# Striking the eight largest scores of a vector with one mask over all vectors, and taking the next tile's maxima one turn earlier

## The reference, cut to what matters

```python
sim = jnp.einsum('pbnhd,hkpd->pbnhk', q, keys)      # 2 x 8 heads x 32 keys for each token
sx, ix = jax.lax.top_k(sim[0], 16)
sy, iy = jax.lax.top_k(sim[1], 16)
all_scores = (sx[..., :, None] + sy[..., None, :]).reshape(b, n, 8, 16 * 16)
scores, pk_indices = jax.lax.top_k(all_scores, 16)
```

## Time and profile before

| | |
|---|---|
| median of 3 runs | 288.17 us (287.86 to 289.52) |
| profiled execution, its own time | 289.14 us |
| span of its trace | 287.4 us |
| DVE busy | 267.8 us, 93% of the span |
| ACT busy | 238.1 us, 83% |
| PE busy | 236.8 us, 82% |
| POOL busy | 229.2 us, 80% |
| mean granted TensorE clock | 0.984 of full speed |

### The profile page before, as it was taken

One profiled execution on the slowest core, in us unless ns is written; L12 is line 12 of the kernel. 1 busy time (PEld: TensorE's weight loads), 2 busy tenths in 40 slices (PEclk: granted clock), 3 DMA queues, 4 the chain that ended last, 5 costly groups with the idle time before them and its releaser, 6 DMA issues.

```text
span 287.4 us, 7837 instructions
## 1 busy us (share of the span) xinstructions
PE 236.8 (82%) x1496; PEld 168.9 (59%) x1496; DVE 267.8 (93%) x2574; ACT 238.1 (83%) x1063; POOL 229.2 (80%) x351
## 2 busy tenths in 40 slices
PE   0699987797989888988898889888988898888781
PEld 0624343485757666766676657665766576656571
DVE  5779999989999999999999999999999999999465
ACT  3248568569898999899989998999899999997843
POOL 7986710376688879997999799979997999798792
PEclk9999999978899999999999999999999999999998
DMA  7920000000000000100010001000100010001002
GB/s 170 275 69 1 1 3 0 0 3 0 2 2 1 2 2 1 39 3 1 1 40 1 1 2 39 5 0 2 38 2 2 3 36 1 5 1 34 7 0 73
DMA packets 11234, 6.27 MB, mean 22 GB/s; under 512 B 1457, under 2 KB 10674, under 8 KB 11186
## 3 DMA queue, kind: packets, MB, share of 16 engines
q1 hardware_dynamic: 9858, 5.12, 6.8%
q10 hardware_dynamic: 1328, 0.66, 1.1%
HBM read 3.67 MB, written 2.10 MB: 20 GB/s over the span
## 4 chain that ended last, share of the span: by engine, by line
DVE 71%; POOL 9%; issue 7%; PE 6%; ACT 3%; DMA 2%; ACTq 0%; POOLq 0%; DVEq 0%
DVE rest L1121 26%; DVE top L1110 14%; DVE top L1130 14%; DVE last L1154 6%; DMA fwq_sb<-in_L_ffn_Wq 2%; DVE slot_gap L1139 2%; DVE sel_m L1173 2%; POOL squareT L487 1%; PE sim L1419 1%; DVE st L1045 1%; DVE sel_a L1176 1%; DVE sel_b L1176 1%; POOL y L578 1%; POOL past L472 1%; POOL wgt L500 1%
## 5 line engine op out<-in xcount | busy, mean ns | idle before, releaser
L1121 DVE MATCH_REPLACE8 rest<-top,sim 128x32 f32<-128x32 f32 x512 | 86.2, 185 | 0.0
L1130 DVE MAX8 top<-rest 128x8 f32<-128x32 f32 x512 | 53.7, 183 | 0.7
L1110 DVE MAX8 top<-sim 128x8 f32<-128x32 f32 x496 | 51.3, 194 | 2.6 <-PE sim L1456 2.6
L807 ACT ACTIVATE prob<-drop 128x50 f32<-128x50 f32 x232 | 53.6, 258 | 0.0
L807 ACT ACTIVATION_READ_ACCUMULATOR prob<-drop 128x1 f32 x232 | 49.1, 216 | 0.0
L1121 DVE MATCH_VALUE_LOAD rest<-top,sim 128x8 f32 x512 | 43.3, 85 | 0.3
L487 POOL TENSOR_TENSOR squareT<-sideT 100x512 bf16<-100x512 bf16 x31 | 32.3, 1042 | 14.2 <-ACT sideT L722 14.2
L472 POOL TENSOR_TENSOR past<-gap,last 128x400 f32<-128x400 f32 x31 | 26.8, 865 | 11.2 <-DVE last L1154 11.1
L1456 PE MATMUL sim<-sim_w,xT_all 128*128 128x512 f32 x64 | 34.4, 620 | 0.8 <-ACT xT_all L756 0.8
L494 POOL TENSOR_TENSOR drop<-gap,out_by 128x400 f32<-128x400 f32 x31 | 32.1, 1034 | 1.8 <-ACT out_by L713 1.7
L1474 PE MATMUL t_bank<-gaps_of,topT 128*128 128x200 f32 x128 | 30.0, 358 | 2.0 <-ACT topT L727 2.0
(11 more groups left out here) (274 smaller groups left out, 713.8 us busy)
## 6 DMA issues: line engine op xcount, KB each, us to landing
out<-y_sb SPq DMA_DIRECT2D x7, 256.0 KB, 2.3
x_sb<-in_L_attn_hidden_states SPq DMA_DIRECT2D x2, 256.0 KB, 4.1
fwq_sb<-in_L_ffn_Wq ACTq DMA_DIRECT2D x2, 256.0 KB, 6.3
x_sb<-in_L_attn_hidden_states SPq DMA_DIRECT2D x1, 512.0 KB, 5.8
wc_sb<-in_L_attn_Wc SPq DMA_DIRECT2D x1, 256.0 KB
out<-last_y SPq DMA_DIRECT2D x2, 128.0 KB, 1.8
wo_in<-in_L_attn_Wo SPq DMA_DIRECT2D x1, 192.0 KB
keys_sb<-in_L_ffn_keys ACTq DMA_DIRECT2D x1, 128.0 KB, 3.7
```

What stands on the lines that cost most here:

```text
L807: last = nc.scalar.activation(prob[d][:, h, :], drop[:, h, :], ACT.Exp, scale=-1.0, accum_out=den[d][:, h:h + 1])
L1110: last = nc.vector.max(top[d][:, v, 0:8], sim_bank[d][:, bass.ts(v, KEYS)])
L1121: last = nc.vector.match_replace(out=rest[:, v, :], in_to_replace=top[d][:, v, 0:8], in_values=sim_bank[d][:, bass.ts(v, KEYS)], imm_value ...
L1130: last = nc.vector.max(top[n % 2][:, v, 8:16], rest[:, v, :])
```

## The change

Of each tile the 16 MATCH_REPLACE8 go. In their place VectorE makes one mask for all 16 vectors (1 where a score is at or over the vector's eighth largest, `mark_above`) and adds mask times -1e38 to the scores (`strike_above`). That strikes too many where scores tie with the eighth. So PE counts the struck scores: `count_above` is four matmuls with the identity that sum the mask from 32 columns a vector to 8, into the tile's own score bank, and VectorE sums these eight (`sum_above`). From the count two small instructions (`spill_above`, `put_ties`) fill 8 more columns of `rest` with the eighth score where a tie was struck, and with a very low number elsewhere; `next_8` reads 40 columns a vector in place of 32.

The order changes as well. `first_8` and `mark_above` of tile n + 1 are issued in VectorE's turn n, `scores` runs one tile further ahead on PE, and `top` has three buffers. `invert_sums` and the threshold steps move within the turn. In the head, `count_above(0)` stands on PE behind `expert_parts`, `count_above(1)` behind `logits(6)`, `count_above(2)` ahead of `pair_gaps(1)` and `count_above(3)` between `transpose_masks` and `count_ranks`. No transfer is added, removed or moved.

```diff
-            def strike_8(n, q):
...
-                for v in range(q * VECS // 4, (q + 1) * VECS // 4):
-                    last = nc.vector.match_replace(out=rest[:, v, :], in_to_replace=top[d][:, v, 0:8],
-                                                   in_values=sim_bank[d][:, bass.ts(v, KEYS)],
-                                                   imm_value=NO_SCORE)
...
+            def mark_above(n):
+                dve.wait_ge(sim_top8, n + 1)
+                if n >= 1:
+                    dve.wait_ge(above_counted, n)
+                nc.vector.tensor_tensor(above[:, :, :], sim_bank[n % 2][:, :].rearrange("p (v k) -> p v k", k=KEYS),
+                                        eighth(n, KEYS), ALU.is_ge).then_inc(above_done, 1)
+            def strike_above(n):
+                dve.wait_ge(above_done, n + 1)
+                if n >= 1:
+                    dve.wait_ge(top_done, 2 * n)
+                nc.vector.scalar_tensor_tensor(rest[:, :, 0:KEYS], above[:, :, :], STRUCK,
+                                               sim_bank[n % 2][:, :].rearrange("p (v k) -> p v k", k=KEYS),
+                                               ALU.mult, ALU.add).then_inc(struck, 1)
+            def sum_above(n):
+                dve.wait_ge(above_counted, n + 1)
+                if n >= 1:
+                    dve.wait_ge(spill_done, n)
+                nc.vector.tensor_reduce(n_above[:, :], sim_bank[n % 2][:, 0:VECS * KEYS // PART].rearrange(
+                    "p (v q) -> p v q", v=VECS), AX_X, ALU.add).then_inc(sim_used, 1)
+            def spill_above(n):
+                dve.wait_ge(sim_used, n + 1)
+                if n >= 1:
+                    dve.wait_ge(ties_done, n)
+                nc.vector.scalar_tensor_tensor(spill[:, :, :], n_above[:, :].unsqueeze(2).to_broadcast([P, VECS, 8]), 2.0,
+                                               rank_row[:, 7:15].unsqueeze(1).to_broadcast([P, VECS, 8]),
+                                               ALU.mult, ALU.subtract).then_inc(spill_done, 1)
+            def put_ties(n):
+                dve.wait_ge(spill_done, n + 1)
+                nc.vector.scalar_tensor_tensor(rest[:, :, KEYS:KEYS + 8], spill[:, :, :], SPILL, eighth(n, 8),
+                                               ALU.mult, ALU.min).then_inc(ties_done, 1)
...
             def first_turn(n):
+                strike_above(n)
+                if n != 2:
+                    first_8(n + 1)
                 if n >= 1:
                     gaps_of_pairs(n - 1)
-                next_8(n, 1)
+                sum_above(n)
+                if n != 2:
+                    mark_above(n + 1)
+                spill_above(n)
                 if n >= 1:
                     gaps_of_thirds(n - 1)
+                put_ties(n)
+                if n >= 1:
                     last_gaps(n - 1)
+                next_8(n, 0)
+                next_8(n, 1)
                 if n == 0:
                     row_stats(6)
                     row_stats(7)
...
             def turn(n):
                 b, j = divmod(n, TB)
+                strike_above(n)
+                if n + 1 in tiles:
+                    first_8(n + 1)
                 if j == 0:
                     maxima(b - 1)
+                sum_above(n)
+                invert_sums(n - 4)
+                spill_above(n)
+                if n + 1 in tiles:
+                    mark_above(n + 1)
+                put_ties(n)
...
+            def count_above(n):
+                pe.wait_ge(above_done, n + 1)
+                pe.wait_ge(struck, n + 1)
+                parts = above[:, :, :].rearrange("p v (q j) -> p j (v q)", j=PART)
+                for j in range(PART):
+                    last = mm(sim_bank[n % 2][:, 0:VECS * KEYS // PART], ident16[:, :], parts[:, j, :],
+                              start=(j == 0), stop=(j == PART - 1))
+                last.then_inc(above_counted, 1)
...
                 if j == 0:
                     project_values(b - 1)
                     top_columns(n - 1)
+                    count_above(n)
                     window_scores(b - 1)
...
-                    scores(n + 1)
+                    scores(n + 2)
...
                 if b == 2:
                     expert_parts()
+                    count_above(0)
                 if b == 3:
+                    scores(2)
                     top_columns(0)
                 if b == 4:
                     pe.wait_ge(gaps_of_done, 1)
                     pair_gaps(0)
-                    scores(2)
+                if b == 6:
+                    count_above(1)
                 if b + 2 < B:
                     transpose_rows(b + 2)
             product.then_inc(z_ready, 1)
+            scores(3)
             top_columns(1)
+            count_above(2)
             pair_gaps(1)
-            scores(3)
...
-            scores(4)
             transpose_masks()
+            count_above(3)
             project_window(0, U_VW, wv_sb)
             count_ranks()
             transpose_sides(1)
+            scores(5)
             project_blocks(0)
```

More of the change, by code:

```diff
@@ L213, in program @@
         s_norm = [sb(f"s_norm{i}", [P, TB, D]) for i in range(2)]
-        top = [sb(f"top{i}", [P, VECS, TOPK]) for i in range(2)]
-        rest = sb("rest", [P, VECS, KEYS])
+        top = [sb(f"top{i}", [P, VECS, TOPK]) for i in range(3)]
+        above = sb("above", [P, VECS, KEYS], BF16)
+        rest = sb("rest", [P, VECS, KEYS + 8])
+        n_above = sb("n_above", [P, VECS])
+        spill = sb("spill", [P, VECS, 8])
         topT = sb("topT", [P, 2 * P])
@@ L1280, in turn @@
                 else:
-                    first_8(n)
-                    invert_sums(n - 4)
-                    strike_8(n, 3)
-                    strike_8(n, 0)
                     gaps_of_pairs(n - 1)
-                    strike_8(n, 1)
+                    next_8(n, 0)
                     gaps_of_thirds(n - 1)
-                    next_8(n, 0)
-                    strike_8(n, 2)
                     last_gaps(n - 1)
                     next_8(n, 1)
+            first_8(0)
+            dve.wait_ge(x_in[3], 16)
+            row_stats(4)
+            row_stats(5)
+            mark_above(0)
             for n in range(TB):
```

107 lines of the change are left out of this document (37 added, 70 removed).

## The result

The changed kernel takes 316.95 us (median of 4 runs, 313.95 to 318.46) against 288.01 for the one before on the same chip (4 runs, 287.72 to 289.52): a ratio of 1.0962, 95% interval 1.0915 to 1.1009. I had said 294.4, and 288 to 301. The direction was right, the size was not. The profiled execution has a span of 313.8 us against 287.4, so 26.4 us have to be found.

What follows compares the result with a forecast made beforehand. VectorE was taken to set the pace, ScalarE 1.5 us behind. Head +11.3, clock +1, rows -3.4, end -1.7, and 1 off for overlapping waits gave +6.2 us: 295.3 profiled, 294.4 as median, range 288 to 301.

Steps and rivals of the forecast that it cites:

- VectorE's new instructions, uncontended: Steady state: new VectorE work costs 1.93 us a tile, 0.74 less than before, making a batch row 25.9 us.
- The port: Steady state: `spill_above` and `put_ties` wait for GpSimd's running SBUF instruction, 0.30 us each in the mean, 2.4 a row.
- The row as VectorE's work and 0.1 for waits: Steady state: a batch row takes about 28.4 us, 0.5 less than now, 3.4 us saved over turns 5 to 31.
- A whole turn lies between it and its next use: Steady state: `invert_sums` moves about 1 us later and GpSimd's `weigh` goes later too, with a turn of slack.
- step 1: Head: VectorE waits 2.6 us at `sum_above(0)` for `count_above(0)`; row statistics end at 31.25, not 26.76.
- steps 2 and 4: Head: 2, late norms make `gaps_of_pairs(0)` wait 2.7 us; 4, the chain behind `next_8(1)` makes VectorE wait 2.0.
- step 3: Head: `count_above(1)`, behind `logits(6)`, is done at 39.4, so `sum_above(1)` waits 3.0 us more.
- The end: End of the kernel: VectorE has `first_8(5)` behind it already and saves 1.7 us.
- The first: Rival, batch rows: engines block each other, a row takes 29.4 us or more, about 301; chance 0.25 with the last rival.
- The port never bites: Rival, batch rows: small instructions settle in GpSimd's gaps, row 27.6 us, about 289, no change; chance 0.14.
- the head isn't on the path: Rival, head: first maxima come only 3 to 4 us later; with a 27.6 us row, -6, 282; chance 0.11.
- twice the time a column: Last rival, VectorE: compare and strike cost 1.13 us each, row 30 or more; chance 0.25 together with the first rival.

Runs made afterwards that it cites:

- kernel 1: Changed kernel with the count's sum and the spill kept in the tile's PSUM score bank, and `scores` waiting for `ties_done`: 317.81 us.
- kernel 6: Changed kernel without `sum_above`, `spill_above` and `put_ties`; `count_above` stays on TensorE with its waits: 316.20 us.
- kernel 5: Changed kernel without any tie handling (`count_above`, `sum_above`, `spill_above`, `put_ties` left out): 286.07 us, 0.984 of the kernel before.
- kernel 11: kernel 5 with four more bf16 matmuls a turn (`transpose_sides` issued twice) and no new wait: 285.26 us.
- kernel 7: Changed kernel without `count_above` on TensorE; VectorE keeps sum, spill and `put_ties`, the sum reading the scores: 304.12 us.
- kernel 2: Changed kernel with `invert_sums(n - 4)` moved from behind `sum_above(n)` to directly behind `strike_above(n)`: 323.46 us.
- kernel 10: Kernel before, its strikes replaced by mask, count and ties all on VectorE, sum and spill in SBUF: 302.39 us, against 291.86 with them in PSUM.
- kernels 4 and 12: 4: changed kernel with `row_stats(6)` and `(7)` ahead of `sum_above(0)`, 310.49 us; 12: the same plus `count_above(1)` issued earlier, at `b == 4`, 307.28 us.

## Why the prediction was wrong

The forecast was +6.2 us, the profiled difference 26.4, so 20.2 are missing: 16.1 in the batch rows, 1.4 in the head, 1.7 at the end, 1.0 taken off for nothing.

- **VectorE's new instructions, uncontended: right.** Mark and strike 0.68 us each, 0.60 to the next; sum 0.28, `next_8` 57.1 / 512 = 112 ns each. With the spill in PSUM a row of VectorE's work is 26.53, where I had 25.9: 0.6 too little.
- **The port: the mechanism right, the moment wrong, the size right by luck.** I took a start at a random moment and one running instruction as the most that is waited for, 2.4 us a row over eight instructions. It came to 29.11 - 26.53 = 2.6, but all from the spill. The order repeats each row, so the same two turns of four were hit (in six of seven rows with nearly the same waits), and one of them waited through three instructions: 2.25 and 1.10 us where 0.29 is the bare price. Most of the lost time is not there: kernel 1 took these waits away and gained 0.14 a row, with the reserve on its own new wait made above.
- **The row as VectorE's work and 0.1 for waits, with the count taken as covered: this is the step that failed.** I had 28.4, the 28.3 and 0.1 for waits. A full-clock row took 30.27 with VectorE busy 29.11: 0.8 of the missing 1.9 is work and port (the two bullets above), and 1.1 is waiting, 1.16 in place of 0.1. Nor is VectorE's work what sets the row: kernel 1 has 26.53 of it in 30.13, kernel 6 has 23.52 in 29.50. The ground for the 0.1 was that the count "ends some 0.7 + 0.4 us into VectorE's turn, while VectorE comes to `sum_above` only behind `first_8(n + 1)`", and that this covers it with about 1 us. It does. I had asked who waits for the count's result. I named the queue behind it, `window_scores`, `pair_gaps` and `scores`, and gave its delay no price. Kernels 5, 6 and 11 show that the count's waits cost 1.6 us of each row where VectorE has no tie handling, and that sixteen matmuls a row without them cost nothing. In the changed kernel itself the count costs less, 0.54 a row (kernel 7), and not by a long stand at the count. These are TensorE's waits and VectorE's for the count, from 108 to 291 us:

```profile
PE c_bank L1541 <- POOL wgt L523: 16.0, 12, 1.6
...
PE sim L1480 <- DVE rest L1135: 0.8, 2, 0.4
...
DVE n_above L1144 <- PE sim L1480: 1.4, 3, 0.8
```

  TensorE stood 0.8 us in all for the strike, and VectorE 1.4 for the count. TensorE's long stand is the one for GpSimd's `wgt`, and it isn't shorter without the count: kernel 7 has 18.8 us of it from 100 to 280 us. So how the count's 0.54 comes into the row, and what makes the rest of its waits, stays open. Over 6.75 rows the missing 1.87 is 12.6 us, and with the 3.3 us of lower clock below that is 15.9 of the 16.1.
- **"A whole turn lies between it and its next use": wrong.** `weigh` waited 18.2 us for the reciprocal over about six rows, and TensorE 16.0 for `wgt`. But moving the reciprocal up left a full-clock row at 30.15 and cost time by the clock (kernel 2), so this was a sign of the ring more than its cause.
- **The row from VectorE's busy time: wrong in method.** The changed kernel takes work from one engine only, and adds waits to a chain that runs from one turn to the next through four queues. Kernel 5 has 5.4 us less on VectorE for 1.0 less in the row; so with the ties left out the whole idea gives 1 to 2% (0.984 of before, 0.988 with kernel 11).
- **The clock in the batch rows: not in the sum.** Eleven times in the rows TensorE waited 1.3 us or more for `wgt` (1.6 at most), and three of these waits, in three rows, were followed 1.4 to 2.1 us later by a stretch at 1.2 GHz. The first of them:

```profile
125.00:126.00 1.00, 0.10 (x1) 0.11 (x2) 1.00 (x10) 1.00 (x10) 0.92 (x3) 1.00 0.00 0
127.00:128.00 1.00, 1.00 (x11) 0.94 (x12) 1.00 (x8) 0.29 (x1) 0.92 (x1) 0.61 0.00 0
128.00:129.00 1.00, 1.00 (x9) 1.00 (x7) 1.00 (x12) 0.78 (x2) 1.00 (x3) 0.50 0.00 0
```

Three rows at 0.89, 0.95 and 0.95 are 1.6, 0.9 and 0.8 over 30.27: 3.3 of the 12.7 us, and somewhat more, because the last row has less work than the others (it took 27.9 where they took 28.9 in the kernel before). Why the other eight waits left the clock as it was isn't known.
- **The head: steps 1, 2 and 4 right or nearly, 3 too small.** VectorE's wait of step 1 was 3.1, forecast 2.6. ScalarE's `norm_rows(7)` stands at 34.02 (I had it end with `take_gaps(0)` at 36.2; `gaps_of_pairs(0)` starts at 36.08):

```profile
34.02 1.65 ACT L694 ACTIVATE xn_all<-x_sb,nmr,rstd 128x128 f32<-128x128 f32 x4 [3.52 <-POOL nmr L453]
...
36.08 0.34 DVE L1174 TENSOR_TENSOR slot_gap<-t_bank,gap 128x176 f32<-128x176 f32 x1 [2.64 <-ACT gap L742]
...
42.33 0.29 DVE L1144 TENSOR_REDUCE n_above<-sim 128x16 f32<-128x128 f32 x1 [5.91 <-PE sim L1480]
...
48.84 0.34 DVE L1174 TENSOR_TENSOR slot_gap<-t_bank,gap 128x176 f32<-128x176 f32 x1 [2.02 <-ACT gap L742]
```

  The waits of steps 2 and 4 are 2.64 and 2.02, forecast 2.7 and 2.0. That of step 3 is 5.91, forecast 3.0: TensorE's half clock fell into it. The two pairs of `logits` matmuls and the transposes and count around them, at twice their length, come to about the 2.9 between the two; I had put 1 us (0 to 4) for the clock. From `select_tokens` (52.24) to the first maxima it took 25.5, forecast 26.0. The walk did not add up exactly in itself: its 8 us, 2.1 and 1.8 would be 11.9, where I wrote 11.3. The 1 us off for waits that fall together was not there. Most of the head's delay hangs on the count too: with the count alone (kernel 6) the first maxima stand at 76.20, without ties (kernel 5) at 64.63.
- **The end: wrong.** I took 1.7 off. `first_8` of the last tile is taken ahead, but the 22.1 us behind the last maxima stayed as they were. No kernel tested what sets them.
- **The rivals.** The first, with rows of 29.4 and more, came nearest. Its words, that no queue can take up the other's jitter, are close to what the waits look like, but its ground was the port, and its price of 0.5 a row too small. "The port never bites" is refuted by kernel 10, "the head isn't on the path" by the first maxima at 77.75 and by kernels 4 and 12, which gave 6.5 and 3.2 us back, and "twice the time a column" by the 0.68 us.

## What to carry to other kernels

When a step is handed to another engine and its result comes back, don't only ask whether the result is there in time. Ask what stands in that engine's queue behind the wait: a wait of up to 1 us a row in a queue through which the next turn passes cost 1.6 us of every row (kernel 6), while similar work without a wait was free (kernel 11). And don't take the time that an engine stands at a semaphore for the price of the step: in the changed kernel TensorE stood 0.8 us over six rows for the strike, and leaving the count out (kernel 7) made each full-clock row 0.54 us shorter and brought the first maxima 5.8 us forward. Where four engines are within some 13% of each other, price a change by the ring from one turn to the next, not by the busiest engine: test it by leaving the whole new part out, then putting back its work and its wait one at a time.

## What the runs showed of the hardware

- A VectorE instruction with two SBUF inputs can be passed over by GpSimd instructions that begin after it: 0.29 us of work took 2.25, through the rest of one and all of two more, and got in at a pause of 0.08.
- Two VectorE instructions of which the second reads what the first wrote start 0.12 us further apart than independent ones (0.72 and 0.60 behind a 128x512 step, 0.33 and 0.21 behind a 128x128 one).
- Behind a hole of 4.17 us TensorE came back at 1.2 GHz in the head, and in three batch rows it fell to that level 1.4 to 2.1 us after a wait of 1.33 to 1.39 had ended, while eight waits of 1.33 to 1.65 were followed by no such fall. Four bf16 matmuls more in each turn neither lengthened a row (27.91 both) nor lowered the clock: kernel 11 has a mean of 0.985, kernel 5 without them 0.968.
